# A graph-attention layer: matmuls of 258, 256 and 257 columns, the row ends' reciprocals one unit earlier, and a start with its first block in halves

## What is computed

```python
def _L0_gnn_ref(h, adj, W_w, W_b, a):          # h: 8192 x 256, adj: 8192 x 8192 of 0 and 1
    Wh = h @ W_w + W_b
    e = leaky_relu((Wh @ a1)[:, None] + (Wh @ a2)[None, :], negative_slope=0.2)
    attention = softmax(where(adj > 0, e, NEG), axis=1)
    return attention @ Wh

h = maximum(layernorm(x), 0.0)
return x + _L0_gnn_ref(h, adj, W_w, W_b, a)
```

## Time and profile before

| | us |
|---|---|
| median of three runs | 1473.85 (1473.39 to 1473.98) |
| profiled execution, its own time | 1475.45 |
| its span, first to last instruction | 1473.7 |
| mean granted TensorE clock | 0.995 |
| TensorE busy / VectorE busy / ScalarE busy | 1443.2 / 1428.4 / 1123.5 |
| first and last L920 matmul start | 107.18 / about 1469 |

### The profile page before, as it was taken

The page is one execution under the profiler, slowest core; times in us unless marked ns, Lnnn a source line. Parts: engine busy times, 40 slices in busy tenths (PEclk is TensorE's granted clock), DMA queues, the critical chain, the costliest instruction groups (busy, mean ns, idle before and its releaser), DMA issues.

```text
span 1473.7 us, 30065 instructions
## 1 busy us (share of the span) xinstructions
PE 1443.2 (98%) x12702; PEld 1272.5 (86%) x12702; DVE 1428.4 (97%) x1232; ACT 1123.5 (76%) x1096; POOL 921.4 (63%) x1232
## 2 busy tenths in 40 slices
PE   6989999999999999999999999999999999999998
PEld 4868888788888888888888888888888888888887
DVE  8989999999999999999999999999999999999996
ACT  5868888687778777697787877787777877778781
POOL 4758344357964499356974489555983679646800
PEclk9989999999999999999999999999999999999999
DMA  9749977594496919996297926988097944968030
GB/s 217 86 40 98 83 54 53 42 106 35 71 102 67 87 21 97 77 92 53 50 102 64 101 31 77 90 79 73 16 116 58 108 37 69 102 68 79 28 59 30
DMA packets 179575, 107.53 MB, mean 73 GB/s; under 512 B 20081, under 2 KB 176369, under 8 KB 179441
## 3 DMA queue, kind: packets, MB, share of 16 engines
q0 software_dynamic: 163296, 82.90, 67.5%
q1 hardware_dynamic: 16144, 22.71, 5.5%
HBM read 298.45 MB, written 8.42 MB: 208 GB/s over the span
## 4 chain that ended last, share of the span: by engine, by line
DVE 70%; issue 14%; PE 13%; ACT 3%; DVEq 0%; DMA 0%; POOL 0%; SPq 0%; ACTq 0%
DVE work L744 31%; DVE work L737 24%; PE acc L920 12%; DVE adj_cols L663 9%; DVE xr L521 1%; DVE X L568 1%; ACT xr L449 1%; ACT work L431 1%; ACT work L416 0%; PE acc L878 0%; PE acc L903 0%; DVE xr L532 0%; DVE xr L563 0%; DVE xr L553 0%; DVE xr L844 0%
## 5 line engine op out<-in xcount | busy, mean ns | idle before, releaser
L920 PE MATMUL acc<-X,work 128*128 128x257 f16 x12288 | 1357.1, 273 | 9.4 <-ACT xr L449 4.5
L920 PEld LDWEIGHTS acc<-X,work 128*128 128x128 f16 x12288 | 1203.8, 98 | 162.8 <-issue 10.5
L303 POOL DMA_DIRECT2D adj_rows<-in_adj x1024 | 555.8, 571 | 430.0 <-DVE adj_cols L663 407.8
L431 ACT ACTIVATE work<-work 128x2048 f16<-128x2048 f32 x254 | 484.4, 1911 | 183.0 <-PE acc L920 100.4
L744 DVE SCALAR_TENSOR_TENSOR work<-work 128x2048 f16<-128x2048 f32 x254 | 605.6, 2384 | 10.5 <-ACT work L431 10.3
L737 DVE SCALAR_TENSOR_TENSOR work<-work,sigma,adj_cols 128x2048 f32<-128x2048 f32 x254 | 591.5, 2329 | 11.5 <-ACT work L416 8.0
L416 ACT ACTIVATE work<-q_odd,r_j 128x1024 f32<-128x1024 f32 x256 | 279.7, 1140 | 34.1 <-DVE work L744 33.6
L416 ACT ACTIVATE work<-work,r_j 128x1024 f32<-128x1024 f32 x252 | 275.1, 1140 | 32.2 <-DVE work L744 31.8
L663 DVE STREAM_TRANSPOSE adj_cols<-adj_rows 128x512 int32<-128x512 int32 x256 | 176.5, 699 | 1.2 <-PE acc L907 1.2
L318 POOL TENSOR_SCALAR part_mean<-mean_hw,rows_without_edge 128x256 f32<-128x256 f32 x56 | 167.1, 2984 | 8.6 <-POOL xr L320 8.4
L320 POOL TENSOR_TENSOR xr<-xr,part_mean 128x256 f32<-128x256 f32 x56 | 128.3, 2292 | 4.7
(11 more groups left out here) (88 smaller groups left out, 154.0 us busy)
## 6 DMA issues: line engine op xcount, KB each, us to landing
adj_rows<-in_adj POOLq DMA_DIRECT2D x1024, 64.0 KB, 7.5
xr<-in_L_gnn_W_b POOLq DMA_DIRECT2D x16, 512.0 KB, 13.9
out<-xr SPq DMA_DIRECT2D x15, 512.0 KB, 4.0
work<-in_x SPq DMA_DIRECT2D x28, 256.0 KB, 15.3
xr<-in_x POOLq DMA_DIRECT2D x14, 512.0 KB, 8.8
work<-q_rows SPq DMA_DIRECT2D x4, 512.0 KB, 6.2
q_odd<-q_rows SPq DMA_DIRECT2D x4, 512.0 KB, 6.2
work<-in_x SPq DMA_DIRECT2D x8, 128.0 KB, 3.2
```

The lines of the kernel that those rows point to most:

```text
L303: pool.dma_start(rows8[QP * q:QP * (q + 1), n % R8], adj_v[s, m, k, q]).then_inc(s_rows[n % R8], 16)
L431: nc.scalar.mul(Et[:, at:at + 2, 0, :], Wt[:, i % RING], SCALE).then_inc(s_H, 1)
L920: return nc.tensor.matmul(acc[:, m, 0:F1], Et[:, 2 * (k % RING) + e, 1 if n == 2 else 0, m * P:(m + 1) * P], X16[:, 2 * k + e, 1 if n == 1 ...
```

## The change

1. **Columns.** The low part of `c_j` moves from column F of the low half of `X16` to column F1 of the high half. The three matmuls now take 258 (features, both denominator columns), 256 (features) and 257 columns. The sum of widths stays 771. `finish` and `finish_last` gain one instruction each time, a `tensor_reduce` that adds the two denominator columns.
2. **Row ends.** In `chunk_after_last`, `finish(…, 0)` goes ahead of unit 3's `weights` and transpose, `finish(…, 1)` ahead of unit 4's `weights`.
3. **The start.** `h_sum` and `hb` go to where VectorE waited for `top`; their matmuls ahead of the eight idle ones; three more idle matmuls are added earlier (`keep_busy`). The first block's product, weights, high and low are made in two halves of 512, TensorE starts on four tiles after the first half. `x_low` of blocks 61 to 63 and the two transposes of the next chunk go later. `q_spread` lies in `work`.

```diff
-        q_spread = cols8[0:QP, 1].rearrange("p w i e -> p (w i e)").bitcast(F32)[:, 4 * F:4 * F + R].rearrange("p (z c e) -> p z c e", c=QP, e=4)
+        q_spread = work[0:QP, (2 * RING + EB - 1) * R:(2 * RING + EB) * R].rearrange("p (z c e) -> p z c e", c=QP, e=4)
...
+            def first_product(b, lo, hi, q, done):
+                nc.scalar.mul(Wt[:, b // 2, b % 2, lo:hi], q[:, lo:hi], r_j[:, b:b + 1]).then_inc(done, 1)
...
             act.wait_ge(s_qp, 1)
-            first_product(0, q_first, s_W0)
-            first_product(1, q_first, s_W)
-            first_high(0, s_M0, 1, s_H0)
+            first_product(0, 0, R // 2, q_first, s_W0)
+            act.wait_ge(s_qp, 2)
+            first_product(0, R // 2, R, q_first, s_W0)
+            first_high(0, 0, R // 2, s_M0, 1, s_H0)
+            first_high(0, R // 2, R, s_M0, 2, s_H0)
+            first_product(1, 0, R, q_first, s_W)
             act.wait_ge(s_q, 16)
-            first_product(2, q_bc[0], s_W0)
-            first_high(1, s_M, 1, s_H)
-            first_product(3, q_bc[0], s_W)
-            first_high(2, s_M0, 2, s_H0)
+            first_product(2, 0, R, q_bc[0], s_W0)
+            first_high(1, 0, R, s_M, 1, s_H)
+            first_product(3, 0, R, q_bc[0], s_W)
+            first_high(2, 0, R, s_M0, 3, s_H0)
             product(0, 2)
-            first_high(3, s_M, 2, s_H)
+            first_high(3, 0, R, s_M, 2, s_H)
             high(0, 2)
             product(0, 3)
             product(0, 4)
...
             dve.wait_ge(s_extT, 1)
             step(nc.vector.tensor_reduce(sc[0:2, 21:22], ps_top[0:2, 0:P], AX.X, ALU.max))
             nc.vector.tensor_scalar(sc[0:2, 22:24], ident[0:2, 0:2], sc[0:2, 21:22], None, ALU.mult).then_inc(s_dg, 1)
-            x_low(NB - 3)
+            dve.wait_ge(s_hT, KF * PAIRS)
+            step(nc.vector.tensor_reduce(h_sum[:, :], hs, AX.X, ALU.add))
+            for c in range(KF):
+                ins = nc.vector.tensor_scalar(hb[:, c * P:(c + 1) * P], ones, h_sum[:, c:c + 1], 1.0 / N, ALU.mult, ALU.mult)
+            ins.then_inc(s_hb, 1)
             dve.wait_ge(s_top, 1)
...
             dve.wait_ge(s_rf, 1)
-            x_low(NB - 2)
-            x_low(NB - 1)
-            dve.wait_ge(s_hT, KF * PAIRS)
-            step(nc.vector.tensor_reduce(h_sum[:, :], hs, AX.X, ALU.add))
-            for c in range(KF):
-                ins = nc.vector.tensor_scalar(hb[:, c * P:(c + 1) * P], ones, h_sum[:, c:c + 1], 1.0 / N, ALU.mult, ALU.mult)
-            ins.then_inc(s_hb, 1)
+            dve.wait_ge(s_tot, 1)
+            nc.vector.tensor_copy(mean[:, :], ps_mean[:, 0:F]).then_inc(s_mean, 1)
+            x_low(NB - 3)
             dve.wait_ge(s_cexp, PAIRS)
             step(nc.vector.tensor_copy(X16[:, :, 0, F], c_j[:, :]))
-            nc.vector.tensor_tensor(X16[:, :, 1, F], c_j[:, :], X16[:, :, 0, F], ALU.subtract).then_inc(s_den, 1)
-            dve.wait_ge(s_qp, 1)
-            for m in range(AHEAD - SETS):
-                transpose(1, m)
-            dve.wait_ge(s_tot, 1)
-            nc.vector.tensor_copy(mean[:, :], ps_mean[:, 0:F]).then_inc(s_mean, 1)
+            nc.vector.tensor_tensor(X16[:, :, 0, F1], c_j[:, :], X16[:, :, 0, F], ALU.subtract).then_inc(s_den, 1)
...
-                step(nc.vector.tensor_scalar(rden[:, lo:lo + H], acc[:, lo:lo + H, F], TINY, None, ALU.max))
+                step(nc.vector.tensor_reduce(rden[:, lo:lo + H], acc[:, lo:lo + H, F:F2], AX.X, ALU.add))
+                step(nc.vector.tensor_scalar(rden[:, lo:lo + H], rden[:, lo:lo + H], TINY, None, ALU.max))
...
                 low(g, 1)
+                finish(g // NC - 1, 0)
                 weights(g, 3)
                 turn(g, 1)
-                finish(g // NC - 1, 0)
+                finish(g // NC - 1, 1)
                 weights(g, 4)
-                finish(g // NC - 1, 1)
                 weights(g, 5)
...
+                nc.vector.scalar_tensor_tensor(out=Et[:, b, 1, lo:hi], in0=Wt[:, b // 2, b % 2, lo:hi], scalar=SCALE,
+                                               in1=Et[:, b, 0, lo:hi], op0=ALU.mult, op1=ALU.subtract).then_inc(done, 1)
+            first_weights(0, 0, R // 2, s_W0, 1, s_M0)
+            first_weights(0, R // 2, R, s_W0, 2, s_M0)
+            first_low(0, 0, R // 2, s_H0, 1, s_E0)
+            x_low(NB - 2)
+            x_low(NB - 1)
+            first_low(0, R // 2, R, s_H0, 2, s_E0)
+            first_weights(1, 0, R, s_W, 1, s_M)
+            first_weights(2, 0, R, s_W0, 3, s_M0)
+            first_low(1, 0, R, s_H, 1, s_E)
+            first_weights(3, 0, R, s_W, 2, s_M)
+            first_low(2, 0, R, s_H0, 3, s_E0)
+            transpose(1, 0)
             weights(0, 2)
-            first_low(3, s_H, 2, s_E)
+            first_low(3, 0, R, s_H, 2, s_E)
+            transpose(1, 1)
             low(0, 2)
...
-                step(nc.vector.tensor_scalar(rden[:, m:m + 1], acc[:, m, F:F1], TINY, None, ALU.max))
+                step(nc.vector.tensor_reduce(rden[:, m:m + 1], acc[:, m, F:F2], AX.X, ALU.add))
+                step(nc.vector.tensor_scalar(rden[:, m:m + 1], rden[:, m:m + 1], TINY, None, ALU.max))
...
+            def keep_busy(n):
+                for i in range(n):
+                    nc.tensor.matmul(ps_q[:, 1, 0:F], ident, Wx[:, i % KF, 0:F], start=True, stop=True)
+            pe.wait_ge(s_X, NB - 4)
+            keep_busy(2)
             pe.wait_ge(s_ext, 1)
             nc.tensor.matmul(ps_top[0:2, 0:P], ext[:, :], ident, start=True, stop=True).then_inc(s_extT, 1)
+            keep_busy(1)
             pe.wait_ge(s_dg, 1)
             nc.tensor.matmul(ps_top[:, P:P + 2], ones[0:2, :], sc[0:2, 22:24], start=True, stop=True).then_inc(s_top, 1)
-            for n in range(WARM):
-                nc.tensor.matmul(ps_mean[:, 0:F], ident, Wx[:, n % KF, 0:F], start=True, stop=True)
-            pe.wait_ge(s_qm, 1)
-            pe.wait_ge(s_X, NB - 4)
-            for h in range(2):
-                ins = nc.tensor.matmul(ps_q[:, h, :], ones[0:QP, :], q_spread[:, 4 * h:4 * h + 4].rearrange("p z c e -> p (z c e)"),
-                                       start=True, stop=True)
-            ins.then_inc(s_qp, 1)
             pe.wait_ge(s_hb, 1)
             for c in range(KF):
                 ins = nc.tensor.matmul(ps_mean[:, 0:F], hb[:, c * P:(c + 1) * P], Wx[:, c, 0:F], start=(c == 0), stop=(c == 1))
             ins.then_inc(s_tot, 1)
-            pe.wait_ge(s_mean, 1)
-            pe.wait_ge(s_X, NB)
-            pe.wait_ge(s_den, 1)
+            keep_busy(WARM)
+            pe.wait_ge(s_qm, 1)
+            for h in range(2):
+                nc.tensor.matmul(ps_q[:, h, :], ones[0:QP, :], q_spread[:, 4 * h:4 * h + 4].rearrange("p z c e -> p (z c e)"),
+                                 start=True, stop=True).then_inc(s_qp, 1)
...
+            WIDTH = (F2, F, F1)
...
-                return nc.tensor.matmul(acc[:, m, 0:F1], Et[:, 2 * (k % RING) + e, 1 if n == 2 else 0, m * P:(m + 1) * P],
-                                        X16[:, 2 * k + e, 1 if n == 1 else 0, 0:F1], start=first, stop=last)
+                return nc.tensor.matmul(acc[:, m, 0:WIDTH[n]], Et[:, 2 * (k % RING) + e, 1 if n == 2 else 0, m * P:(m + 1) * P],
+                                        X16[:, 2 * k + e, 1 if n == 1 else 0, 0:WIDTH[n]], start=first, stop=last)
...
-            def block_of_unit(k, e, first=False):
-                for m in range(M):
+            def block_of_unit(k, e, lo, hi, first=False):
+                for m in range(lo, hi):
                     for n in range(3):
                         ins = part(m, k, e, n, first=(first and n == 0))
                 return ins
...
+            pe.wait_ge(s_mean, 1)
+            pe.wait_ge(s_den, 1)
+            pe.wait_ge(s_X, NB - 2)
             pe.wait_ge(s_E0, 1)
+            block_of_unit(0, 0, 0, H, True)
+            pe.wait_ge(s_X, NB)
+            pe.wait_ge(s_E0, 2)
             pe.wait_ge(s_W, 1)
-            block_of_unit(0, 0, True)
+            block_of_unit(0, 0, H, M, True)
             pe.wait_ge(s_E, 1)
-            block_of_unit(0, 1)
-            pe.wait_ge(s_E0, 2)
-            block_of_unit(1, 0)
+            block_of_unit(0, 1, 0, M)
+            pe.wait_ge(s_E0, 3)
+            block_of_unit(1, 0, 0, M)
             pe.wait_ge(s_E, 2)
-            block_of_unit(1, 1).then_inc(s_pe, 1)
+            block_of_unit(1, 1, 0, M).then_inc(s_pe, 1)
```

More of the change, by code:

```diff
@@ L459, in _, with first_high @@
             q_first = ps_q.rearrange("p h i -> p (h i)")
-            def first_product(b, q, done):
-                nc.scalar.mul(Wt[:, b // 2, b % 2, :], q, r_j[:, b:b + 1]).then_inc(done, 1)
-            def first_high(b, made, count, done):
+            def first_product(b, lo, hi, q, done):
+                nc.scalar.mul(Wt[:, b // 2, b % 2, lo:hi], q[:, lo:hi], r_j[:, b:b + 1]).then_inc(done, 1)
+            def first_high(b, lo, hi, made, count, done):
                 act.wait_ge(made, count)
```

(34 more changed lines are left out.)

## The result

| | before | changed |
|---|---|---|
| median of five runs, us | 1473.66 (1473.39 to 1473.98) | 1466.23 (1466.04 to 1466.57) |
| profiled execution, own time / span | 1475.45 / 1473.7 | 1466.23 / 1464.4 |

The ratio is 0.9948, 95% interval 0.9934 to 0.9961; a second time, on the chip of the second four experiments, 0.9947 (0.9934 to 0.9959). So 7.4 us less, where the prediction had 8.8 from 1473.85 (1465.1); the profiled executions are 9.2 apart.

A forecast was written before the change was run, and what follows sets the result against it. VectorE and TensorE, nearly equal bounds, meet with ScalarE at group ends. Start -0.4, group ends -2.7 - 1.7 - 2.5, columns -3.0, last tiles +1.5 make -8.8; 1475.45 - 8.8 - 1.6 = 1465.1 us, range 1463.5 to 1469.0.

The forecast's parts named there:

- Row ends, -6.9: Ends of row groups: earlier reciprocals remove TensorE's gaps, -2.7 at the first, -1.7 for the clock's fall, -2.5 later.
- its sum of 168.0 against 168.5: Main part: VectorE needs 168.0 us a group after the change, still below TensorE, so it gains until it waits for tiles.
- Columns, -3.0: Main part's matmuls: two columns go per step, so 256 columns save one step per triple; 7 groups count, -3.0 us.
- columns don't pay: Rival for the matmuls: time is linear in the width, so nothing is saved; +3.0, 1468.1 us, chance 0.20.
- Last tiles, +1.5: Kernel's end: VectorE is already slower than TensorE, so the added reduction is paid 8 times 0.19, +1.5 us (1.0 to 3.2).
- The rival with 0.4 for it: VectorE becomes the bound: reductions cost 0.4 instead of 0.19, VectorE's group takes 168.3; about 1467 us, chance 0.07.
- The start, -0.4: First group: TensorE's first matmul comes near 103.5, but VectorE sets unit 3, at 115.7 for unit 2's `low`; -0.4 us.
- in the bounds: Ends given for the start's gain in the first group: -0.7 and +0.3 us.
- the last line of the sum: Final subtraction: 1475.45 - 8.8 - 1.6 = 1465.1 us, the 1.6 being the profiled execution's excess over the runs' median.
- the clock still falls at the start: Rival at the start: the clock falls under the eight idle matmuls, which then take 5.4 us; 1466.5 us, chance 0.10.

The follow-up runs named there:

- the second four experiments: Second of three sets of four follow-up kernels, each set run on one chip; the kernel before took 1473.80 us on the second chip.
- the group of 254 columns: Changed kernel with another matmul width in each group of rows; the group with 254 columns had a period of 167.79 us, a pace of 108.33 ns.

## Why the prediction was right, and where it was off

**Row ends, -6.9: right**, in mechanism and size, by the run with this part alone and by six periods of 168.53 us in the changed trace. VectorE did reach the last tile before TensorE in the later groups, as its sum of 168.0 against 168.5 said (167.8 by the group of 254 columns), and it costs nothing.

**Columns, -3.0: right.** The step of two columns is measured, and so is that the gain counts only once the row ends are moved. The rival *columns don't pay*, time linear in the width, is excluded. The page TensorE: Matmul & The Clock Gate of the Trainium skill, section Back-to-back issue gap, has that linear rule, N / 2.4 + 2.5 ns. By it 256 and 258 columns take 109.17 and 110.00 ns, as measured, but 255 and 257 columns 108.75 and 109.58, where 109.17 and 110.00 were measured; the measurement decides.

**Last tiles, +1.5: right**: 1.37 became 1.56 us a tile, and a reduction is a step of 0.19 us. The rival with 0.4 for it falls with that.

**The start, -0.4: right against the trace it was read from, wrong against the median.** `last_units` starts 268.84 - 267.93 = 0.9 us earlier; 0.3 of this is the whole execution running earlier from the beginning (the last two `x_low` in a row start at 90.86, before at 91.14). So 0.6, in the bounds. The mechanism held: TensorE's first matmul came 3.9 us earlier and unit 3 only 0.9.

**The step that failed is the last line of the sum**, "1.6 more than the runs' median", subtracted as if it were a constant. The own time was forecast as 1475.45 - 8.8 = 1466.65 and came out at 1466.23. But 1.3 to 1.4 of that 1.6 was the fall of the clock under the idle matmuls. The earlier trace rows showed it, and I named it as a rival for the changed kernel; I didn't ask whether the median of before had it. About three in five executions of before don't, and none of the five behind the median does. For them the start is a loss of 0.8 us, for the sum -6.9 - 3.0 + 1.5 + 0.8 = -7.6, measured -7.4. The rival *the clock still falls at the start* has 1466.5, nearer to the measured 1466.2 than my 1465.1, but by chance: in the changed kernel the idle matmuls ran at full clock, 3.61 us.

For the two clusters of the kernel before there are four traces that sort as their times do, the 1.26 us that can be followed from the start to the end in two of them, and the changed start, which has one cluster in each of the eight kernels that were run with it more than once (57 executions, no cluster wider than 0.6 us). What decides in an execution whether the clock falls there wasn't tried.

## What to carry to other kernels

When two engines are both busy at 97%, find the place where they wait for each other and free it first: the faster matmuls were worth nothing here until then, and their full amount after (a faster VectorE wasn't tried). Where a profiled execution stands off the median of the runs, look for a stretch with a lower granted clock, and ask which of the two courses the sum is made against. Matmuls that only keep TensorE busy are worth 1.9 us here (1466.99 against 1465.09) if they end before the data that the next ones need are there, and cost what they overrun, 1.1 us with eight.

## What the hardware did that was not expected

- Matmul pace with 254 to 260 columns of fp16 is a staircase of 0.83 ns per two columns: 108.33, 109.17, 110.00, 110.83 ns. An uneven width pays for the next even one.
- A `tensor_scalar` on one column of PSUM whose scalar operand is also in PSUM took 0.22 us and 0.26 to the next dependent step, against 0.16 and 0.19 with a constant.
- 3.4 or 6.8 us of half clock at the beginning of the main part gave the same start of group 1's last units, 267.93 and 267.90.
